# Graph attention and mixture of experts on one core: the adjacency matrix cast in the transfer, with GpSimd issuing both halves ahead of its powers

## Chip, cores and metric

The kernel runs on one core of a Trainium2 chip, which it has to itself. The metric is the device time of one execution in microseconds, as the median of several runs. Engines are named as in the profile: PE (TensorE), DVE (VectorE), ACT (ScalarE), POOL (GpSimd), SP (SyncE, which only issues transfers here).

## What is computed

Two layers over x (2048 tokens, 512 wide), each added to its input. The first is graph attention over an adjacency matrix of 2048 x 2048 zeros and ones, with 16 heads of 32:

```python
x = x + gnn(layernorm(x), adj)
x = x + ffn(layernorm(x))          # router, 8 experts (top 2), shared feed-forward part

def gnn(x, adj, W_seq, a1, a2, W_out, b_out):
    seq = (x @ W_seq).reshape(N, H, DH)
    score1 = einsum('nhd,d->hn', seq, a1)
    score2 = einsum('nhd,d->hn', seq, a2)
    scores = leaky_relu(score1[:, :, None] + score2[:, None, :], 0.2)
    attn = softmax(scores + (1.0 - adj)[None] * -65500.0, axis=-1)
    hidden = einsum('hij,jhd->ihd', attn, seq).reshape(N, D_IN)
    return elu(hidden @ W_out + b_out)
```

A row of the adjacency without any neighbour attends to all tokens evenly.

## The kernel before

leaky_relu has two slopes, so the exponential of a score is a product of a factor of the row token and one of the column token, with one pair of factors on either side of zero. For each head the kernel therefore makes a 0/1 mask "score above zero" and adds up, with PE, the masked values with one pair of factors and the unmasked with the other. The mask (fp8, 2048 x 1024 per unit) is ANDed with the adjacency (fp8, holding -1 and 0, `adj8`, as words `adjw`). A unit is one head and one half (1024) of the rows: 32 units, in 8 pairs of heads, k = 0 to 3 within a pair (head k % 2, half k // 2).

**Setup** (up to about 100 us in the profile). SP loads the constants, W (two pieces), x (four groups of four tiles of 128 tokens) and then the adjacency, 32 pieces of 128 x 1024 floats, through five buffers `adj_in` (lines 192 to 207). ACT and DVE cast them to fp8 in turn (`cast`, lines 223 and 356), 16 pieces each. At the same time DVE centres W, takes the row statistics (`stats`), GpSimd raises the variances to -0.5 in four powers (`root`, line 292), PE transposes W and x and projects x (`project`, line 505, 12 products of 512 columns a tile, with a high and a low part of both operands), ACT splits off high parts (`high_x`) and copies the projected tiles scaled by the power (`copy_v`, line 215, which waits for the power of its group), DVE makes the low parts (`low_x`). PE's `scores` makes both scores of a group, `scores_to_tokens` and `scores_to_rows` turn them; ACT copies the rows (line 265), stores them to memory and loads one row spread over all partitions, `s1b` (lines 267 to 273). DVE ORs the adjacency tiles (`any_neighbour`, lines 424 to 428), PE sums these over the partitions (`degrees`, line 550), and DVE writes flags for rows without neighbours into the adjacency (`apply_empty_rows`, lines 435 and 437). Each engine has its own instruction order, written out by hand; semaphores join them.

**Loop** (to 487.86 us). For each unit DVE compares 6 of the 16 column tiles with the row (line 794) and masks them (`mask_own`, line 802), ACT compares the other 10 (a steep sigmoid, line 730), which DVE masks (`mask_acts`, line 809). PE multiplies (lines 956 and 960) once `m_ready` says that the masks are there. DVE collects the sums from PSUM (`collect`, line 816), GpSimd scales and adds them (`combine`, lines 901 and 906). GpSimd also makes the value products of the next heads (`products`, lines 891 and 893), ACT their high part (`split_high`, line 738), DVE the low (`low_values`, line 823). There are four mask buffers, `MB = 4`. In round k, DVE waits for unit k, collects it, compares and masks its own part of unit k+4, and masks ACT's part of unit k+3.

After the loop come the output projection and the second layer, to the end of the kernel; neither is touched.

## Time and profile before

| | us |
|---|---|
| median of 3 runs | 1058.4 (1056.38 to 1060.91) |
| profiled execution | 1060.79 |
| its span | 1058.9 |
| PE busy | 1006.7 (95%) |
| DVE busy | 803.9 (76%) |
| ACT busy | 666.5 (63%) |
| POOL busy | 251.5 (24%) |
| first attention unit begins | 99.76 |
| output projection begins | 487.86 |

Busy times are of the profiled execution. A busy PE is not a PE at its peak, since matmuls overlap. Where a shape stands beside a row, it is partitions x elements. In a timeline an entry in square brackets gives how long the engine was idle before, and what released it. Lines are those of the kernel before.

### The profile page before, as it was taken

The page shows a single profiled execution, that of the slowest core. Times are in us where ns is not written, and L with a number is a line of the kernel's source. Part 1 is how long each engine was busy: PE and PEld are TensorE (multiplying, and loading weights), DVE is VectorE, ACT ScalarE, POOL GpSimd, SP SyncE. Part 2 cuts the span into 40 slices and gives each one's busy share as a digit, 9 for nine tenths or more (in the row PEclk, how much of TensorE's full clock was granted, in tenths as well). Part 3 has the DMA queues.
Part 4 walks back from the last instruction along what each step waited for, and adds up shares of the span by engine and source line. Part 5 has one row for each costly group of instructions (what it writes and reads, how often), then busy time and mean ns, then how long its engine had stood idle before and what let it go on. Part 6 is the DMA issues. An engine that isn't in the chain of part 4 may idle for free.

```text
span 1058.9 us, 27195 instructions
## 1 busy us (share of the span) xinstructions
PE 1006.7 (95%) x11256; PEld 890.0 (84%) x11256; DVE 803.9 (76%) x1197; ACT 666.5 (63%) x990; POOL 251.5 (24%) x271
## 2 busy tenths in 40 slices
PE   5996889999999999999899999999999999989998
PEld 4875889999999999997677888888888877778887
DVE  6776899999999999993699433448775668975554
ACT  2668999999989889933356333344454546655431
POOL 1103124334333443363331000000065000006500
PEclk9996999999999999999899999999999999999999
DMA  8781111111111111623635000020063124453242
GB/s 301 249 313 40 41 62 43 45 61 42 43 52 52 42 43 52 225 67 132 229 116 208 1 1 1 1 80 1 26 207 117 50 80 131 130 158 112 85 134 99
DMA packets 53778, 102.45 MB, mean 97 GB/s; under 512 B 6161, under 2 KB 26257, under 8 KB 53138
## 3 DMA queue, kind: packets, MB, share of 16 engines
q1 hardware_dynamic: 47666, 82.83, 23.6%
q0 software_dynamic: 3072, 8.39, 2.5%
q10 hardware_dynamic: 2928, 9.57, 2.4%
q8 instruction: 90, 1.47, 0.6%
q14 instruction: 22, 0.18, 0.1%
HBM read 74.69 MB, written 26.08 MB: 95 GB/s over the span
## 4 chain that ended last, share of the span: by engine, by line
PE 47%; issue 2%; DVE 2%; DMA 1%; POOL 1%; ACT 0%; SPq 0%; POOLq 0%; DVEq 0%; ACTq 0%
PE bank L1758 16%; PE bank L1291 16%; PE bank L668 3%; PE bank L1835 2%; PE bank L1786 1%; PE bank L1787 1%; PE bank L1789 1%; DMA xs<-sorted_latent_rows 1%; PE bank L1805 1%; PE bank L1779 1%; PE bank L1743 1%; PE bank L1741 1%; PE bank L665 1%; PE bank L1740 1%; DVE acc_rest L1492 0%
## 5 line engine op out<-in xcount | busy, mean ns | idle before, releaser
L730 ACT ACTIVATE arena<-arena 128x1024 fp8e4<-128x1024 f32 x320 | 336.6, 1136 | 2.5 <-ACT arena L722 1.6
L956 PE MATMUL bank<-arena 128*128 128x132 f16 x4096 | 285.6, 222 | 19.0 <-DVE arena L816 7.6
L956 PEld LDWEIGHTS bank<-arena 128*128 128x128 fp8e4 x4096 | 246.6, 98 | 20.8 <-issue 8.6
L1291 PE MATMUL bank<-xt,up_parts 128*128 128x512 f32 x768 | 186.2, 391 | 0.0
L1758 PE MATMUL bank<-down_parts,h_parts 128*128 128x512 f32 x768 | 184.5, 389 | 0.1
L960 PE MATMUL bank<-arena 128*128 128x66 f16 x4096 | 173.5, 196 | 0.0
L794 DVE TENSOR_SCALAR arena<-arena 128x1024 uint8<-128x1024 f32 x192 | 167.8, 940 | 2.7 <-DMA arena<-s_rows 2.7
L1758 PEld LDWEIGHTS bank<-down_parts,h_parts 128*128 128x128 f32 x768 | 143.9, 188 | 30.5 <-issue 0.5
L1291 PEld LDWEIGHTS bank<-xt,up_parts 128*128 128x128 f32 x768 | 142.3, 188 | 28.6 <-ACT relu_sb L1240 0.2
L960 PEld LDWEIGHTS bank<-arena 128*128 128x128 fp8e4 x4096 | 154.9, 98 | 0.0
L1265 DVE TENSOR_TENSOR relu_sb<-relu_sb 128x512 f32<-128x512 f32 x64 | 44.4, 693 | 118.0 <-ACT relu_sb L1240 110.9
L1240 ACT ACTIVATE relu_sb<-bank 128x512 f32<-128x512 f32 x64 | 38.3, 598 | 148.6 <-PE bank L1291 143.8
L901 POOL TENSOR_TENSOR arena<-arena 128x264 f32<-128x264 f32 x64 | 43.1, 694 | 214.3 <-DVE arena L809 195.5
L809 DVE TENSOR_TENSOR arena<-arena 128x2560 uint32<-128x2560 uint32 x32 | 90.2, 2819 | 2.6 <-ACT arena L730 2.5
L1259 ACT CAST down_parts<-down_sb 128x512 fp32r<-128x512 f32 x64 | 39.9, 623 | 72.4 <-PE bank L1758 66.7
L1712 POOL DMA_INDIRECT sorted_latent_rows<-latent,slot_idx x32 | 35.0, 1094 | 208.7 <-DVE slot_idx L1578 190.9
L1280 DVE TENSOR_TENSOR down_parts<-down_sb,down_parts 128x512 fp32r<-128x512 f32 x64 | 44.2, 691 | 50.1 <-ACT down_parts L1259 46.8
L1724 POOL DMA_INDIRECT y_gathered<-sorted_expert_rows,slot_idx x32 | 32.6, 1020 | 156.3 <-DMA sorted_expert_rows<-expert_y 135.4
L891 POOL TENSOR_TENSOR arena<-arena 128x512 f32 (+1 forms) x32 | 50.2, 1569 | 59.3 <-ACT arena L220 31.4
L802 DVE TENSOR_TENSOR arena<-arena 128x1536 uint32<-128x1536 uint32 x32 | 56.3, 1758 | 1.1
L816 DVE TENSOR_REDUCE arena<-bank 128x198 f32<-128x396 f32 (+1 forms) x96 | 44.2, 516 | 9.8 <-PE bank L956 9.8
L668 PE MATMUL bank<-wo_parts,hT 128*128 128x512 f32 x192 | 50.2, 412 | 0.0
(231 smaller groups left out, 1403.9 us busy)
## 6 DMA issues: line engine op xcount, KB each, us to landing
hid<-in_adjT SPq DMA_DIRECT2D x32, 512.0 KB, 5.8
arena<-s_rows SPq DMA_DIRECT2D x30, 512.0 KB, 3.7
sorted_latent_rows<-zeros SPq DMA_DIRECT2D x1, 4992.0 KB, 18.5
xs<-sorted_latent_rows SPq DMA_DIRECT2D x39, 128.0 KB, 2.1
sorted_expert_rows<-expert_y SPq DMA_DIRECT2D x39, 128.0 KB, 1.7
arena<-in_x SPq DMA_DIRECT2D x4, 1024.0 KB, 10.8
xr<-in_x SPq DMA_DIRECT2D x16, 256.0 KB, 2.8
up_sb<-in_upT ACTq DMA_DIRECT2D x1, 4096.0 KB, 14.0
```

The lines of the kernel that those rows point to most:

```text
L668: last = nc.tensor.matmul(bank[2 + t % 2][:, :], hT[:, t % 2, a, k, :], wo_parts[:, b, k, :], start=False, stop=(n == len(terms) - 1))
L730: last = nc.scalar.activation(m8[:, k, j, :], s1b[:, k % 2, :], ACT.Sigmoid, bias=bias_now[:, k % 2, j:j + 1], scale=STEEP, saturate=False)
L794: last = nc.vector.tensor_scalar(mu8[:, k, j, :], s1b[:, k % 2, :], neg_s2[:, 2 * p + k % 2, j:j + 1], float(ONE8), ALU.is_gt, ALU.mult)
L802: nc.vector.tensor_tensor(mw[:, k, 0:DVE_J, :], mw[:, k, 0:DVE_J, :], adjw[:, 0:DVE_J, cols], ALU.bitwise_and).then_inc(own_masked, 1)
L809: nc.vector.tensor_tensor(mw[:, k, DVE_J:, :], mw[:, k, DVE_J:, :], adjw[:, DVE_J:, cols], ALU.bitwise_and).then_inc(m_ready, 1)
L816: last = nc.vector.reduce_sum(sums[:, k % 2, t0:t0 + n, :], bank[3 * (k % 2) + g][:, 0:n * WV].rearrange("p (t s c) -> p t c s", t=n, s=2) ...
L891: nc.gpsimd.tensor_tensor(vtmp[:, :, c * W1:c * W1 + DH], vh, val[:, :, bass.ds(h, 1)].to_broadcast([P, T, DH]), ALU.mult)
L956: last = nc.tensor.matmul(o, m8[:, k, j, i * P:(i + 1) * P], vs[:, b, j, :], start=(j == 0), stop=(j == T - 1))
L960: nc.tensor.matmul(od, adj8[:, ja, (k // 2) * IC + i * P:(k // 2) * IC + (i + 1) * P], vs[:, b, ja, :].rearrange("p (s c) -> p s c", s=2)[ ...
L1265: nc.vector.tensor_tensor(r, r, r, ALU.mult).then_inc(sq_ready, 1)
L1291: last = nc.tensor.matmul(bank[6 + s % 2][:, :], sa[:, s % 2, a, k, :], xt[c][:, b, k, :], start=(i == 0), stop=(i == len(mm) - 1))
L1758: last = nc.tensor.matmul(ob[t][:, :], hhl[:, s % 2, a, t * P:(t + 1) * P], sb_[:, s % 2, b, :], start=(n == 0 and (a, b) == TERMS[0]), st ...
```

## The change

The setup is rewritten around a transfer that casts, and the loop's order shifts by one unit.

- The adjacency is no longer loaded as floats and cast. GpSimd, after its constants and a wait for the second group of x (`x_loaded[1]`), issues eight transfers that read floats and write fp8 straight into `adj8`: 512 rows by 1024 columns each, first the four of the first half of the columns, then the four of the second, and only then its four powers. `cast`, `adj_in` and all semaphores of the casts are gone. The adjacency now holds +1 and 0; the flags set the sign bit everywhere and -1 in rows without neighbours.
- SP loads W in four pieces and x in groups of 2, 2, 4, 4 and 4 tiles; the small constants are issued by ACT. W is centred by ACT, piece by piece, and transposed piece by piece.
- The rows of scores go to memory in three stores issued by SP. The first holds only what the first two heads need of the first half; the two spread rows are loaded right behind it.
- PE's order: `scores_to_rows` ahead of `project(7)`, `degrees(1)` ahead of `project(13, 14, 15)`. Unit 0 begins with the first 12 token tiles (`T_A = 12`) of three of its row tiles, the last 4 follow; the values of the first head are made in two parts, 12 tiles by GpSimd and 4 by DVE.
- DVE applies the empty rows of the first half before the first compare, and in the loop compares three units ahead (not four) and masks ACT's part two ahead (not three). ACT's compares shift likewise. In the first pair the mask buffers are used in the order 0, 2, 1, 3.

The core of the diff:

```diff
-            for q in range(HALVES):
-                if q >= AB:
-                    sp.wait_ge(cast_by_act if (q - AB) % 2 else cast_by_dve, (q - AB) // 2 + 1)
-                sp.dma_start(adj_in[:, q % AB, :], adjT[(q % T) * P:(q % T + 1) * P, (q // T) * IC:(q // T + 1) * IC]
-                             ).then_inc(adj_loaded[q % AB], 16)
+            sp.wait_ge(st_copied, 6)
+            sp.dma_start(s1_dram[0:2, 0:IC], s1_rows[0:2, 0:IC]).then_inc(s1_stored, 16)
+            sp.wait_ge(s1_stored, 16)
+            for k in range(2):
+                sp.dma_start(s1b[:, k, :], s1_dram[k:k + 1, 0:IC].to_broadcast([P, IC])).then_inc(s1_staged[k], 16)
...
+            def load_adjacency(half):
+                cols = slice(half * IC, (half + 1) * IC)
+                for g in range(AG):
+                    pool.dma_start(adj8[:, 4 * g:4 * g + 4, cols],
+                                   adjT[512 * g:512 * g + 512, cols].rearrange("(j p) i -> p j i", p=P)
+                                   ).then_inc(adj_loaded[half], 16)
+
+            pool.wait_ge(x_loaded[1], 16)
+            load_adjacency(0)
+            load_adjacency(1)
             for g in range(4):
                 root(g)
...
-                cast_up_to(8)
+                dve.wait_ge(adj_loaded[half], 16 * AG)
                 step(nc.vector.tensor_tensor(anyw, adjw[:, 0:4, words], adjw[:, 4:8, words], ALU.bitwise_or))
...
+            high_x(0, 1, 2, 3)
             copy_v(0)
-            high_x(2, 3)
             act.wait_ge(wa_in_psum, 1)
             nc.scalar.copy(wa[:, :, 0:2 * H], WA_BANK[:, 0:KD * 2 * H].rearrange("p (k s) -> p k s", k=KD)).then_inc(wa_high, 1)
...
-            project(8, 9, 10, 11, 12, 13, 14, 15)
+            project(8, 9, 10, 11, 12)
             degrees(1)
+            project(13, 14, 15)
...
-                        if k or not first:
-                            dve.wait_ge(unit_in_psum, 4 * p + k + 1)
-                            collect(p, k)
-                        if not last:
-                            if k >= 2:
-                                low_values(p + 1, k % 2)
-                            compare(p + 1, k)
-                            mask_own(p + 1, k)
-
-                        if k == 0:
-                            mask_acts(p, 3)
-                        elif not last:
-                            mask_acts(p + 1, k - 1)
+                        dve.wait_ge(unit_in_psum, 4 * p + k + 1)
+                        collect(p, k)
+                        if not last and k >= 2:
+                            low_values(p + 1, k % 2)
+                        if not last or k == 0:
+                            compare(p + (k + 3) // 4, (k + 3) % 4)
+                            mask_own(p + (k + 3) // 4, (k + 3) % 4)
+                        if not last or k < 2:
+                            mask_acts(p + (k + 2) // 4, (k + 2) % 4)
...
                 dve.wait_ge(seq_in_psum, 8)
                 compare(0, 0)
-                cast(26)
                 mask_own(0, 0)
-                cast(28, 30)
                 any_neighbour(1)
-                low_values(0, 0)
-                mask_acts(0, 0)
-                dve.wait_ge(seq_in_psum, T)
                 compare(0, 1)
                 mask_own(0, 1)
+                mask_acts(0, 0)
+                low_first(0, slice(0, T_A))
+                apply_empty_rows((2,))
+                products_first(slice(T_A, T))
+                low_first(1, slice(T_A, T))
+                apply_empty_rows((3,))
+                compare(0, 2)
+                mask_own(0, 2)
                 low_values(0, 1)
                 mask_acts(0, 1)
```

## Rows read from the trace of the kernel before

**Rows 1.** windows of setup and loop: busy us by engine, clock, DMA share, GB/s
```profile
0.00:99.70 99.70, 76.20 (x384) 62.13 (x384) 67.82 (x122) 59.74 (x83) 11.65 (x19) 0.94 0.70 239
...
150.00:430.00 280.00, 276.68 (x6132) 275.80 (x6130) 279.18 (x275) 267.24 (x268) 108.63 (x120) 1.00 0.14 48
```

**Rows 2.** PE's timeline: start us, us, line, operation, count
```profile
17.82 0.47 PE L511 MATMUL bank<-w_high,x_high 128*128 128x512 f32 x1 [1.08 <-DVE x_low L353]
...
31.02 0.40 PE L511 MATMUL bank<-w_high,x_high 128*128 128x512 f32 x1
...
33.75 1.47 PE L502 MATMUL bank<-arena 128*128 128x128 f32 x12
...
99.76 0.27 PE L956 MATMUL bank<-arena 128*128 128x132 f16 x1 [7.23 <-DVE arena L809]
...
106.63 0.67 PE L960 MATMUL bank<-arena 128*128 128x66 f16 x16
...
108.07 0.67 PE L960 MATMUL bank<-arena 128*128 128x66 f16 x16
...
487.86 0.73 PE L665 MATMUL bank<-bout_parts,ones_r 1*128 1x512 f32 x2
```

**Rows 3.** waits, 60 to 100 us: waiter, awaited, us, times, longest
```profile
POOL arena L891 <- ACT arena L220: 31.4, 1, 31.4
```

**Rows 4.** groups up to 99 us: line, operation, count, busy, mean ns
```profile
L227 ACT ACTIVATE arena<-hid 128x1024 fp8e4<-128x1024 f32 x16 | 16.7, 1056 | 3.5 <-DMA hid<-in_adjT 3.1 <-ACT arena L265 0.5
...
L361 DVE TENSOR_SCALAR arena<-hid 128x1024 fp8e4<-128x1024 f32 x16 | 10.8, 687 | 0.8 <-DMA hid<-in_adjT 0.8
...
L437 DVE TENSOR_TENSOR arena<-arena 128x2048 uint32<-128x2048 uint32 x2 | 4.6, 2293 | 0.1
...
L424 DVE TENSOR_TENSOR hid<-arena 128x1024 uint32<-128x1024 uint32 x2 | 2.4, 1219 | 0.0
...
L435 DVE TENSOR_SCALAR arena<-bank 128x512 uint8<-128x512 f32 x2 | 1.4, 683 | 0.0
```

**Rows 5.** DVE's timeline: the first compare, and four rounds of the loop
```profile
74.38 4.07 DVE L794 TENSOR_SCALAR arena<-arena 128x1024 uint8<-128x1024 f32 x6 [2.69 <-DMA arena<-s_rows]
...
201.65 1.38 DVE L816 TENSOR_REDUCE arena<-bank 128x198 f32<-128x396 f32 x3
202.95 1.34 DVE L823 TENSOR_TENSOR arena<-arena 128x1056 f16<-128x1056 f32 x1
204.21 6.08 DVE L794 TENSOR_SCALAR arena<-arena 128x1024 uint8<-128x1024 f32 x6
210.33 1.76 DVE L802 TENSOR_TENSOR arena<-arena 128x1536 uint32<-128x1536 uint32 x1
212.00 2.82 DVE L809 TENSOR_TENSOR arena<-arena 128x2560 uint32<-128x2560 uint32 x1
214.74 1.38 DVE L816 TENSOR_REDUCE arena<-bank 128x198 f32<-128x396 f32 x3
...
226.17 1.38 DVE L816 TENSOR_REDUCE arena<-bank 128x198 f32<-128x396 f32 x3
...
238.24 1.38 DVE L816 TENSOR_REDUCE arena<-bank 128x198 f32<-128x396 f32 x3
...
248.62 1.38 DVE L816 TENSOR_REDUCE arena<-bank 128x198 f32<-128x396 f32 x3
```

**Rows 6.** windows of the transfers, columns as in rows 1
```profile
5.00:25.00 20.00, 12.41 (x76) 11.65 (x77) 15.69 (x40) 5.17 (x9) 2.07 (x2) 1.00 1.00 382
...
25.00:62.00 37.00, 37.00 (x208) 30.36 (x208) 28.07 (x57) 24.18 (x38) 3.75 (x5) 1.00 0.75 236
```

**Rows 7.** GpSimd's first power, and its nearest transfer (ns min/median/max)
```profile
14.84 1.05 POOL L294 TENSOR_TENSOR arena<-arena 128x4 f32<-128x4 f32 x1 [13.63 <-DVE arena L346]
...
L1712 POOL DMA_INDIRECT sorted_latent_rows<-latent,slot_idx x32: 959/970/1502, 764.9 to 816.4; - x32
```

**Rows 8.** ACT's timeline: the issue of the store of the rows
```profile
61.06 0.40 ACTq L267 DMA_DIRECT2D s_rows<-arena  x1
```

More of the change, by code:

```diff
@@ L256, in setup_act @@
-            cast(11)
+            copy_scores(3)
             copy_v(5)
-            copy_scores(3)
-            cast(13, 15)
+            copy_rows(0, 1)
             copy_v(6)
-            cast(17)
-            copy_v(7)
-            for c in range(4):
-                act.wait_ge(st_in_psum, 5 + c)
-                nc.scalar.copy(s1_rows[:, c * 512:(c + 1) * 512], ROW_BANK[c][0:H, :]).then_inc(st_copied, 1)
-            act.wait_ge(st_copied, 8)
-            act.dma_start(s1_dram[:, :], s1_rows).then_inc(s1_stored, 16)
@@ L268, in setup_act @@
-            cast(19)
-            copy_v(8)
-            cast(21)
-            act.wait_ge(s1_stored, 16)
-            for k in range(2):
-                act.dma_start(s1b[:, k, :], s1_dram[k:k + 1, 0:IC].to_broadcast([P, IC])).then_inc(s1_staged[k], 16)
-            copy_v(9)
+            copy_rows(2, 3)
             act.wait_ge(expin_ready, 1)
@@ L347, in stats @@
                                         ALU.add).then_inc(var_ready, 1)
+            def stats(g):
+                row_stats(*range(4 * g, 4 * g + 4))
+                variances(g)
             def low_x(*tiles):
@@ L354, in low_x @@
                                             xhi[:, t, :, :].bitcast(f32), ALU.subtract).then_inc(xl_ready, 1)
-            def cast(*even):
-                for q in even:
-                    dve.wait_ge(adj_loaded[q % AB], 16 * (q // AB + 1))
-                    src, dst = cast_source(q)
-                    nc.vector.tensor_scalar(dst, src, -1.0, None, ALU.mult, saturate=False).then_inc(cast_by_dve, 1)
             def diagonal_a():
@@ L554, in setup_pe @@
             pe.wait_ge(consts_loaded, 48)
-            pe.wait_ge(w_centred, 1)
-            transpose_w()
+            for c in range(KD):
+                transpose_w(c)
             transpose(0, 1)
-            pe.wait_ge(w_ready, 1)
+            pe.wait_ge(w_ready, KD)
             project(0)
@@ L735, in split_high, with split_first @@
                 def split_high(p, b):
-                    act.wait_ge(prod_ready, 2 * p + b + 1)
+                    act.wait_ge(prod_ready, 2 * p + b + 2)
                     nc.scalar.copy(vs[:, b, :, 0:WD], vtmp).then_inc(hi_copied, 1)
+                def split_first(part, tiles):
+                    act.wait_ge(prod_ready, part + 1)
+                    nc.scalar.copy(vs[:, 0, tiles, 0:WD], vtmp[:, tiles, :]).then_inc(hi_copied, 1)
                 def body(p, last):
                     for k in range(4):
-                        act.wait_ge(unit_in_psum, 4 * p + k + 1)
-                        if not last:
-                            if k >= 2:
-                                split_high(p + 1, k % 2)
-                            compare(p + 1, k)
+                        if not (last and k):
+                            act.wait_ge(unit_in_psum, 4 * p + k + 1)
+                        if not last and k >= 2:
+                            split_high(p + 1, k % 2)
+                        if not last or k == 0:
+                            compare(p + (k + 3) // 4, (k + 3) % 4)
@@ L831, in split_low, with body @@
                     nc.vector.tensor_scalar(ones_r[0:1, :], ident2[0:1, :], 0.0, 1.0, ALU.mult, ALU.add).then_inc(wo_low, 1)
-                def body(p, last=False, first=False):
+                def body(p, last=False):
                     for k in range(4):
@@ L950, in _, with products @@
                         pe.wait_ge(m_ready, 4 * p + k + 1)
-                        for i in range(IT):
+                        def products(i, tokens):
                             g, slot = GROUP_OF[i]
@@ L963, in _ @@
                                         start=False, stop=False, skip_group_check=True)
+                            return last
+                        ahead = [t0 for t0, n in GROUPS] if p == 0 and k == 0 else []
+                        for i in ahead:
+                            if i == ahead[-1]:
+                                pe.wait_ge(v_copied, T - 1)
+                            products(i, range(T_A))
+                        if ahead:
+                            pe.wait_ge(lo_ready, 2)
+                        for i in ahead:
+                            products(i, range(T_A, T))
+                        for i in range(IT):
+                            if i not in ahead:
+                                last = products(i, range(T))
                         last.then_inc(unit_in_psum, 1)
```

326 lines of the change are left out of this document (165 added, 161 removed).

## Prediction, before the changed kernel was run

> **What bounds the kernel now.** I read the stages first, then the chain inside each. The windows by stage show two regimes [rows 1]: up to 99.70 us no engine is full (PE 76.20, DVE 67.82, ACT 59.74 us of it), from 150 to 430 us PE and DVE are both full (276.68 and 279.18 of 280). In the setup the end is set by a chain: 99.76 us is where the first attention unit begins, after 7.23 us of idle PE [rows 2]. Behind it stands GpSimd, which could not multiply the values of the first head before the last tile was copied by ACT: 31.4 us of waiting for line 220 [rows 3]. ACT is late with those copies because PE is late with its 16 projections, and both ACT and DVE also cast the adjacency, 16 halves each [rows 4].
>
> In the loop one unit costs PE eight tiles of 1.44 us (106.63 to 108.07), 11.52 us [rows 2]. DVE's round of collect, compare, mask has four lengths, read from collect to collect [rows 5]: 13.09 (k=2, with low values and with GpSimd's products beside it: its six compares take 6.08), 11.43 (k=3), 12.07 (k=0, products again), 10.38 (k=1). The sum is 46.97 for four units, 0.9 more than PE's 46.1. DVE is the bound on average, and the masks of a unit are finished three units ahead, so a long round is evened out by a short one. The loop ends at 487.86, where the output projection begins [rows 2]. From there both kernels are the same.
>
> **The change part by part.** The times below are on the clock of the profiled run (1060.8 us, span 1058.9). It stands 2.4 over the median of 1058.4, and I take the difference of the sum over to the median.
>
> *Casts.* 16 on ACT at 1.056 and 16 on DVE at 0.687 go: 16.7 and 10.8 us of work [rows 4], none of it on the path by itself while PE is full, but it held up the copies and the order of DVE.
>
> *Start.* W comes in four quarters and first in the queue, its centring goes to ACT, tile by tile. In the new order, with 128x512 on DVE at 0.68 [rows 4]: first quarter of W landed at 4.6, four quarters of statistics of 1.1 to 9.1, the small diagonal and two x statistics to 10.8, four low parts of W to 13.2 at 0.62 apart (ACT's high parts are ready by 11.8), the first low part of x to 14.0. So the first projection is at 14.0, an estimate, instead of 17.82 [rows 2]: -3.8.
>
> *The eight transfers.* GpSimd waits for the second group of x, estimated at 9.4 us: 2 MB behind the first byte at the 382 GB/s of 5 to 25 us [rows 6], begun 1.4 us earlier. Then it issues eight transfers of 512 rows, and only then the first power (1.05) [rows 7]. ACT stands at the copy of tile 0 until that power is there; behind it are the score columns, x tiles 4 and on, so all of PE. PE would want those columns at 25.5: 14.0, two projections of 2.73, the products for the columns (3.6), five tiles of x at 0.4 (twelve transposes in 1.47 [rows 2]) and their waits, 0.4. ACT and DVE take 1.5 from the power to the columns, so the power is wanted at 24.0. So there is cover for 24.0 - 9.4 - 1.05 = 13.5 us of issuing, 1.7 us each. No row shows a direct transfer from GpSimd. The nearest is an indirect one of 128 rows, 0.97 [rows 7]. Bounds: 0.97 (rows cost nothing) and 3.9 (four times as many rows, all in proportion). I take 1.94, double, as part of the 0.97 must be fixed and indices fall away: 15.5 us, 2.0 us over the cover. Below nothing isn't possible: the powers cannot come before their variances at 20.
>
> The row only shows 0.97 for 128 rows. The Trainium skill (DMA: Bandwidth & Descriptors, Anatomy of one DMA) calls descriptor generation small and variable, with many descriptors to be had before the cost shows. By that the 2.0 us would be nothing and the result 1049.0; no run here shows it.
>
> *To the first compare.* From the first projection to the issue of the rows' store it was 61.06 - 17.82 = 43.2 [rows 2, 8], with PE full (37.00 of 37 us [rows 6]). One projection (2.73, 31.02 to 33.75 [rows 2]) now comes later, and two of four row copies, estimated at 0.5 each: 39.5. So the store is issued at 14.0 + 39.5 + 2.0 = 55.5. In the kernel before, it was 13.3 from that issue to the compare at 74.38 [rows 5, 8], beside a busy queue; the store is now a sixteenth of the size and I take 10: 65.5. On DVE the empty rows come before: with a projection and the degrees to go for PE these end near 60.2, two flags of 0.68 + 2.29 [rows 4] behind 59.3, then the scaling, 66.1. So the first compare starts at 66 instead of 74.38.
>
> *From there to round 0 of the loop* DVE has in its order: compare 4.07 and own mask 1.67, three ORs of 1.22, compare and own mask again, mask of ACT's part 2.73, low values of 12 tiles 0.95, an empty-row flag 3.0, products and low values of 4 tiles 1.0, a flag 3.0, third compare beside products 5.7 and own mask 1.67, low values 1.25, ACT's mask 2.73 [rows 4, 5]. That is 37.2. For the handing of the 4 tiles over ACT, and for GpSimd's products beside the second compare, I add 2.2. Round 0 begins at 105.4. PE: projections end near 87, degrees of the second half wait some 2 us for the ORs; unit 0 needs PE from about 89 to 102 and is covered.
>
> *The loop itself changes.* Compares are made three units ahead instead of four, and ACT's part is masked two ahead instead of three. The masks of unit k+2 are finished by round k's last instruction, and round k+1 starts only when unit k+1 is done, a unit that could start only with round k. Rounds and units go in step: each step costs the longer of the two. With 0.14 (estimated) for handing over in the rounds where DVE would be the shorter: 13.09 + 11.66 + 12.07 + 11.66 = 48.5 a pair instead of 46.97. For seven pairs 339.5. From the last pair's start three units (34.6) and 0.9 for eight transposes ahead of the last (twelve take 1.47 [rows 2]): 35.5. End: 105.4 + 339.5 + 35.5 = 480.4, against 487.86: -7.4. **Predicted: 1058.4 - 7.4 = 1051.0.** Gross, the setup gives some 18 us and the loop takes 11 back.
>
> *The data.* 16.8 MB and 3 MB of x from 9.4 us at 382 GB/s: second half landed at 61.5, wanted by DVE at 66 + 5.7 = 71.7; first half near 39, wanted at 43. Covered, while the stream holds 320 GB/s. Bounds: 382, and the 236 of 25 to 62 us [rows 6], where the casts held the transfers back. I take 382, since reading is what fills the engines in those rows (share 1.00).
>
> **The rivals.**
> *B, the powers come late (0.16).* At 3.9 us each, 31.2 us of issuing is 17.7 over the cover, 15.7 more than forecast: 1066.7. It decides from 1.7 us each; the gain is gone at 2.9. For it: 512 rows against 128, ACT in order. Against: the fixed part. The Trainium skill (SBUF — State Buffer, Who interferes with whom) adds that GpSimd can't write descriptors while DVE runs a two-port operation. Here DVE's compares are longer beside GpSimd's products (6.08 against 4.07 [rows 5]), so the two do hinder each other; in the window of issuing DVE mostly reads PSUM or makes statistics.
>
> *C, the casting stream is slower than the plain one (0.20).* At 236 GB/s the second half lands at 93.7, 22 us behind its want: 1058.4 - 7.4 + 22 = 1073. It decides under 320 GB/s and the gain is gone at 290. For it: no row shows a casting transfer. Against: the rows written are a quarter of those read. This is the slower side in its clearest form.
>
> *D, no stepping (0.13).* If DVE's rounds even out after all (less contention, since PE idles and ACT has less to do), the loop keeps 46.97 a pair: 1040.
>
> *E, the clock falls in the loop (0.07).* In step, PE idles 1.6 us in each pair. After the stall before 99.76 three tiles took 6.87 (99.76 to 106.63) instead of 4.32 [rows 2], and the granted clock was 0.94 over that stage, 1.00 in the loop [rows 1]. If each such gap does the same: 7 x 2.55 = 17.9, 1068.9. Against: PE's gaps of 0.9 in a pair today leave the clock at 1.00.
>
> **How the numbers follow.** The forecast has 0.44, with 1046 to 1057 as its own range (issuing 1 to 2.4 us, first compare give or take 4). 0.5% is 5.3 us and about what a measurement of this kernel can tell from no change. Faster by more (under 1053.1): two thirds of the forecast, all of D: 0.45. Within (to 1063.7): the rest of the forecast, mild forms of B, C and E: 0.27. Slower: 0.28, strong forms of B, C and E. The range that leaves out 2 in 10 goes from D to just under C: 1040 to 1072.
>
> **What would show it.** In the profile after: the first power of GpSimd near 26 and ACT's copy of tile 0 right behind it (B: near 40); DVE not waiting for the adjacency at the first OR (C: a wait on the transfer of in_adjT, of some 20 us at the second half); first compare near 66, unit 0 near 89; collects of DVE in the loop 13.1, 11.7, 12.1, 11.7 apart with short waits for PE (D: 47.0 in four); granted clock 1.00 from 150 to 430 (E: lower); output projection at 480. A new wait that none of these has, say DVE for the copied tiles in the second half of the setup, would make the sum wrong.

## Result

| | before | after |
|---|---|---|
| median | 1058.72 us (1056.38 to 1062.01, 9 runs) | 1064.05 us (1062.19 to 1065.14, 9 runs) |
| profiled execution | 1060.79 | 1063.28 |
| its span | 1058.9 | 1061.5 |
| first projection | 17.82 | 13.38 |
| first compare on DVE | 74.38 | 69.19 |
| first attention unit begins | 99.76 | 90.00 |
| output projection begins | 487.86 | 491.83 |

The ratio is 1.0041, with an interval of 1.0027 to 1.0056. 1051.0 was predicted, so the sign was wrong. The attention begins 9.8 us earlier and ends 4.0 us later. Behind the output projection the two profiled executions differ by 1.5 us (572.9 and 571.5), with nothing changed there; the medians are 5.3 us apart.

Two stages of the changed kernel, the start of the loop and the steady loop, in the columns of [rows 1]:

```profile
88.00:150.00 62.00, 52.50 (x1058) 51.49 (x1057) 54.61 (x58) 58.33 (x60) 18.55 (x21) 0.92 0.13 43
150.00:430.00 280.00, 267.51 (x5865) 265.86 (x5864) 264.59 (x261) 251.50 (x250) 99.91 (x111) 0.99 0.13 44
```

In the loop neither PE (267.51) nor DVE (264.59) is full any more, where both had all but filled the 280 us before [rows 1]. The waits from 150 to 430 us say why (waiter, awaited, us in all, times, longest):

```profile
DVE arena L816 <- PE bank L965: 13.3, 11, 3.1
ACT arena L722 <- PE bank L965: 13.3, 6, 3.9
PE bank L965 <- DVE arena L809: 12.5, 11, 1.8
```

DVE waits for PE at its collect (line 816), and PE waits for DVE's last mask (line 809), eleven times each: they take turns. DVE's own timeline shows the rounds, from collect to collect (line 816). The first five collects here are the first pair with a wait for ACT in it (line 823), the last is one steady pair later:

```profile
107.80 1.38 DVE L816 TENSOR_REDUCE arena<-bank 128x198 f32<-128x396 f32 x3
122.02 1.39 DVE L816 TENSOR_REDUCE arena<-bank 128x198 f32<-128x396 f32 x3 [3.52 <-PE bank L965]
133.54 1.39 DVE L816 TENSOR_REDUCE arena<-bank 128x198 f32<-128x396 f32 x3 [1.24 <-PE bank L965]
136.81 1.26 DVE L823 TENSOR_TENSOR arena<-arena 128x1056 f16<-128x1056 f32 x1 [1.88 <-ACT arena L730]
...
148.13 1.38 DVE L816 TENSOR_REDUCE arena<-bank 128x198 f32<-128x396 f32 x3
162.65 1.39 DVE L816 TENSOR_REDUCE arena<-bank 128x198 f32<-128x396 f32 x3 [3.07 <-PE bank L965]
...
211.45 1.39 DVE L816 TENSOR_REDUCE arena<-bank 128x198 f32<-128x396 f32 x3 [0.43 <-PE bank L965]
```

From 162.65 to 211.45 a pair takes 48.80 us, against 46.97 before [rows 5], and its four rounds 11.87, 11.95, 13.03 and 11.95. The first pair, 107.80 to 162.65, takes 54.85, and its rounds 14.22, 11.52, 14.59 and 14.52. PE beside it:

```profile
108.03 0.27 PE L965 MATMUL bank<-arena 128*128 128x132 f16 x1 [5.67 <-DVE arena L809]
109.01 1.95 PE L965 MATMUL bank<-arena 128*128 128x132 f16 x16
113.75 1.10 PE L965 MATMUL bank<-arena 128*128 128x132 f16 x16
...
148.36 0.27 PE L965 MATMUL bank<-arena 128*128 128x132 f16 x1 [3.33 <-DVE arena L809]
149.34 1.95 PE L965 MATMUL bank<-arena 128*128 128x132 f16 x16
```

Behind both idle stretches (5.67 and 3.33 us) the same sixteen products take 1.95 instead of 1.10 us: TensorE is at 1.2 GHz there (granted clock 0.50 from 108 to 113) and back at 2.4 from 113 to 115 (0.99). And GpSimd, which was the question of the change:

```profile
10.53 6.22 POOL L304 DMA_DIRECT2D arena<-in_adjT  x8 [9.32 <-DMA arena<-in_x]
21.29 1.04 POOL L293 TENSOR_TENSOR arena<-arena 128x4 f32<-128x4 f32 x1 [4.54 <-DVE arena L349]
...
45.20 0.38 POOL L299 PARTITION_ALL_REDUCE arena<-arena  x1 [5.93 <-issue]
53.70 0.59 POOL L315 TENSOR_TENSOR arena<-arena 128x1 f32<-128x1 f32 x1 [8.12 <-issue]
60.55 0.39 POOL L299 PARTITION_ALL_REDUCE arena<-arena  x1 [6.26 <-issue]
```

Eight issues take 6.22 us together, 0.78 each, and the first power waits 4.54 us for its variances (line 349), not for them. Behind the powers stands what the prediction didn't price: a power, an all-reduce, a power, an all-reduce, with 5.93, 8.12 and 6.26 us between them in which GpSimd waits for nothing that the profile shows. DVE stands behind the last of them:

```profile
60.98 0.43 DVE L403 TENSOR_TENSOR arena<-arena 128x256 f32<-128x256 f32 x1 [7.43 <-POOL arena L299]
...
62.44 0.68 DVE L429 TENSOR_SCALAR arena<-bank 128x512 uint8<-128x512 f32 x1
...
69.19 4.06 DVE L794 TENSOR_SCALAR arena<-arena 128x1024 uint8<-128x1024 f32 x6
```

### The profile page after: what moved, and what is told of

It is laid out like the page before. It is cut to its first block, busy times and chain, and to the rows that moved or that the text cites. A ratio compares the mean times of both kernels' runs of the same rounds, so it can differ in the third digit from the quotient of the medians.

```text
span 1061.5 us, 27178 instructions
## 1 busy us (share of the span) xinstructions
PE 1009.1 (95%) x11256; PEld 889.8 (84%) x11256; DVE 795.0 (75%) x1186; ACT 654.2 (62%) x979; POOL 257.6 (24%) x279
## 4 chain that ended last, share of the span: by engine, by line
PE 46%; issue 2%; DVE 2%; DMA 2%; POOL 1%; ACT 0%; SPq 0%; POOLq 0%; DVEq 0%; ACTq 0%
PE bank L1781 16%; PE bank L1314 16%; PE bank L656 3%; PE bank L1858 2%; DMA xs<-sorted_latent_rows 1%; PE bank L1809 1%; PE bank L1810 1%; PE bank L1812 1%; PE bank L1766 1%; PE bank L1764 1%; PE bank L653 1%; PE bank L1802 1%; PE bank L1828 1%; DMA sorted_expert_rows<-expert_y 1%; PE bank L1763 1%
## 5 line engine op out<-in xcount | busy, mean ns | idle before, releaser
L897 POOL TENSOR_TENSOR arena<-arena 128x512 f32 (+2 forms) x32 | 46.8, 1462 | 40.6 <-ACT arena L221 15.0
```

The source lines that it names most:

```text
L897: nc.gpsimd.tensor_tensor(vtmp[:, tiles, c * W1:c * W1 + DH], vh[:, tiles, :], val[:, tiles, bass.ds(h, 1)].to_broadcast([P, n, DH]), ALU. ...
```

## Experiments

The theory after the result: the setup's gain is real, and the loop's shorter look-ahead takes more than all of it (S). Rivals: the transfers or their order cost it; GpSimd's chain costs it (G); PE's clock costs it (K). All ratios are against the kernel before, measured beside each run on the same chip.

| run | us | ratio (interval) | output projection at |
|---|---|---|---|
| e1 four ahead | 1051.06 | 0.9905 (0.9880 to 0.9929) | 479.90 |
| e2 before, in step | 1076.0 | 1.0142 (1.0115 to 1.0169) | 505.91 |
| e3 reduces together | 1059.7 | 0.9986 (0.9966 to 1.0007) | 486.42 |
| e4 second half behind the powers | 1074.24 | 1.0128 (1.0103 to 1.0152) | |
| e5 four ahead, reduces together | 1046.37 | 0.9852 (0.9821 to 0.9884) | 476.32 |
| e6 fillers | 1063.99 | 1.0029 (1.0015 to 1.0042) | 492.38 |
| e7 before, cast in the transfer | 1053.51 | 0.9926 (0.9901 to 0.9951) | 480.28 |
| e8 second half last | 1074.52, one run | | |
| e9 sixteen transfers | 1065.56, one run | | |
| e10 both halves behind the powers | 1081.51, one run | | |
| e11 layout only | 1064.22 | 1.0035 (1.0009 to 1.0061) | 491.41 |
| e12 e5 with fillers | 1049.12 | 0.9879 (0.9836 to 0.9922) | 477.10 |
| e13 ACT relieved | 1059.23 | 0.9993 (0.9982 to 1.0005) | 486.80 |
| e14 ACT relieved, fillers | 1059.63 | 0.9988 (0.9975 to 1.0002) | 487.98 |

### The look-ahead: e1, e2, e11

e1 is the changed kernel with the loop of the kernel before (its diff in DVE's order; ACT and GpSimd likewise). So that the mask buffers can be used in plain order, x and its parts lie in two halves of eight tiles.

```diff
-BUF = (0, 2, 1, 3)
+BUF = (0, 1, 2, 3)
...
-                            compare(p + (k + 3) // 4, (k + 3) % 4)
-                            mask_own(p + (k + 3) // 4, (k + 3) % 4)
-                        if not last or k < 2:
-                            mask_acts(p + (k + 2) // 4, (k + 2) % 4)
+                            compare(p + 1, k)
+                            mask_own(p + 1, k)
+                        if k == 0:
+                            mask_acts(p, 3)
+                        elif not last:
+                            mask_acts(p + 1, k - 1)
```

> The changed kernel with the loop's look-ahead of before: DVE compares four units ahead and masks ACT's part three ahead, ACT and GpSimd likewise, mask buffers in plain order, for which the x tiles lie in another order in the same memory. The setup is left as changed. Theory S (the shorter look-ahead makes PE and DVE go in step and that takes the setup's gain back): four units take 47.0 us again instead of 48.8, seven pairs give back 12.7 us, the output projection begins near 479 and the time is about 1052, under the kernel before. Rival T (the loss is in the first units and in slower clocks, not in the look-ahead): pairs stay near 48.8 and the time within 2 us of 1064.

Measured 1051.06 us (1048.70 to 1051.49). From 183.20 to 230.16 a pair takes 46.96 us, as before. In the waits of the loop DVE's for PE is gone, and PE waits about as rarely as before (e1, 150 to 430 us):

```profile
PE bank L972 <- DVE arena L821: 4.5, 6, 0.9
```

e2 is the opposite edit, the changed kernel's loop in the kernel before.

> The kernel before with the loop of the changed kernel alone: compares three units ahead, ACT's part masked two ahead; setup untouched. Theory S: four units take 48.8 us instead of 47.0, the first unit stays near 99.8, and the time is 1058.7 + 7 x 1.8 = about 1071 (less, down to 1068, if less DVE work stands ahead of the first units). Rival T: about 1059, no change beyond noise.

Measured 1076.0: 15 us slower by the ratio, 5 over the expected 1071. In the profile 2.4 us of it lie ahead of the loop (the first unit begins at 102.15 instead of 99.76), where nothing was edited; the rest was not followed up. Its loop waits like the changed one's:

```profile
DVE arena L817 <- PE bank L948: 13.7, 12, 3.0
PE bank L948 <- DVE arena L810: 13.7, 11, 1.8
```

e11 has e1's layout of x and the loop of the changed kernel.

> Control for the run with four ahead: the changed kernel with that run's layout of x (two halves of eight tiles, mask buffers in plain order) and its own look-ahead of three. If the gain of 13 us came from the look-ahead, this one stays at 1064, ratio 1.002 to 1.006. If the layout gave it, 1051.

Measured 1064.22 us: the layout does nothing. So one unit of look-ahead is worth 13.0 us in one kernel and about 15 in the other (1.42% of 1060), more than the 11 that the prediction charged, and it alone turns a gain of 1% into a loss. Four ahead doesn't free the start of the loop from ACT, though: in e1 DVE waits 6.76 us for ACT's compares (line 722) ahead of its first collect and 2.22 for its copy (line 730) behind it, against 2.51 us for ACT at this place in the kernel before. What it would give to take that away as well, no run shows.

### The cast by itself: e7

The kernel before with `adj_in` and all casts taken out, and the eight transfers of the change in front of the powers. The flags for empty rows are those of the change; order and loop are those of before.

```diff
-            for q in range(HALVES):
-                if q >= AB:
-                    sp.wait_ge(cast_by_act if (q - AB) % 2 else cast_by_dve, (q - AB) // 2 + 1)
-                sp.dma_start(adj_in[:, q % AB, :], adjT[(q % T) * P:(q % T + 1) * P, (q // T) * IC:(q // T + 1) * IC]
-                             ).then_inc(adj_loaded[q % AB], 16)
...
+            pool.wait_ge(x_loaded[1], 16)
+            load_adjacency(0)
+            load_adjacency(1)
             for g in range(4):
                 root(g)
```

> The kernel before with only the transfer changed: the adjacency read as floats and written as fp8 by eight transfers that GpSimd issues in front of its powers, no casts on ACT and DVE, the flags for empty rows as in the changed kernel. Order of everything else and the loop are those of the kernel before. Theory: the issue of the eight (6.2 us in the changed kernel) ends at 17.7 and the first power comes 2.9 us later than the 14.84 of the kernel before, which PE feels little; without the casts ACT's copies and DVE's order run earlier, so that the first attention unit begins near 93 to 95 instead of 99.76, and as the loop keeps its four units of look-ahead, the whole gain is seen at the end: 1052 to 1054, ratio 0.994 to 0.996. Rival: the setup is bound by the chain of scores, store, broadcast and all-reduces alone, in which no cast lies: first unit near 99, ratio 0.998 to 1.000.

Measured 1053.51 us; the theory holds (the first unit was expected at 93 to 95 and begins at 92.21). The output projection begins at 480.28, e1's at 479.90: all the rest of the rewritten setup, which brings the first projection forward by 4.0 us (17.34 in e7, 13.31 in e1) and takes the store of the rows apart, is worth 0.4 us in these two profiles. The medians lie 2.5 us apart, with intervals of the ratios that overlap. Both stand behind the same link, GpSimd's second all-reduce. Here it is in e7:

```profile
60.35 0.39 POOL L289 PARTITION_ALL_REDUCE arena<-arena  x1 [8.01 <-issue]
```

It begins at 61.41 in e1 and at 60.35 here, and the first compare at 70.06 and 70.17. How much the rest of the setup gives once this link is out of the way was not measured on its own.

### GpSimd's chain: e3, e5

e3 is the changed kernel with both all-reduces next to each other:

```diff
             largest(0, slice(H, H + 1))
+            largest(1, slice(0, H))
             pool.wait_ge(var_ready, 5)
             nc.gpsimd.tensor_tensor(gfac[:, 1:2], gfac[:, 0:1], inv_root, ALU.pow).then_inc(std_ready, 1)
-            largest(1, slice(0, H))
```

> The changed kernel with GpSimd's two all-reduces behind one another and the fifth power (of the scale factor) behind both, instead of between them. Theory G (each change between powers and all-reduces costs GpSimd 6 to 8 us without an instruction, and this chain, not PE, the transfers or the row store, sets DVE's first compare): exponents of DVE begin near 54 instead of 61, the fifth power comes near 61, the first compare starts at 66 to 67 instead of 69.2, the time falls by 2 to 3 us to about 1061.5. Rival: the gaps are the reduce's own latency, whatever stands before it; then the second all-reduce still ends near 61 and the time stays at 1064.

Measured 1059.7 us, 4.3 under the changed kernel, where 2 to 3 were expected. GpSimd in e3:

```profile
52.99 0.55 POOL L299 PARTITION_ALL_REDUCE arena<-arena  x1 [7.07 <-DVE arena L396]
60.95 1.07 POOL L316 TENSOR_TENSOR arena<-arena 128x1 f32<-128x1 f32 x1 [7.41 <-issue]
```

The second all-reduce now waits for its data (line 396) and nothing else, and begins at 52.99, where the rival had it end near 61; the change back to a power, 7.41 us, happens beside DVE's work. The first compare begins at 65.31 instead of 69.19, behind PE's degrees (DVE waits 3.43 us for line 535 ahead of the flags), which is the next link. Whether an all-reduce behind another has a gap of its own is not shown: the wait of 7.07 us is long enough to hide one. e5 puts this edit and the look-ahead of e1 together.

> The changed kernel with both of the earlier edits: the loop's look-ahead of the kernel before (compares four units ahead, own layout of x so that the mask buffers are in plain order) and the two all-reduces back to back with the fifth power behind them. Theory: the two losses lie one behind the other, so the gains add. The look-ahead alone gave 1064.05 - 1051.06 = 13.0, the reduces alone 1064.05 - 1059.7 = 4.3: 1046.8 or a ratio of about 0.987 to 0.988. Rival: the loop of four ahead can absorb a late first round, so that what the first round gains is not seen at the end: 1051, ratio 0.990 to 0.993, as with the look-ahead alone.

Measured 1046.37 us (1044.24 to 1047.16): the gains add, and this beats both kernels, by 1.5% and 1.7%.

### What lengthens the gaps: e4, e8, e10

e4 puts `load_adjacency(1)` behind the four powers, e10 both halves, e8 the second half behind the last all-reduce.

> The changed kernel with the four transfers of the second half issued behind the four powers. Theory: the eight issues took 6.2 us in all and ended 4.5 us before the first power could start, so nothing waits for them; the power stays at 21.3, the second half lands near 60 instead of 57.3, wanted at 75, and the time stays within 1.5 us of 1064. Rival (transfers issued ahead of the powers hold up the x tiles or the powers): faster than the changed kernel by 2 us or more, x groups land earlier.

e4 took 1074.24 us, 10 more than the changed kernel, a miss. Its transfers of the second half are issued from 40.67 to 43.73, and its gaps are longer:

```profile
52.98 0.38 POOL L299 PARTITION_ALL_REDUCE arena<-arena  x1 [9.24 <-issue]
64.88 0.59 POOL L315 TENSOR_TENSOR arena<-arena 128x1 f32<-128x1 f32 x1 [11.53 <-issue]
72.36 0.39 POOL L299 PARTITION_ALL_REDUCE arena<-arena  x1 [6.89 <-issue]
```

The last all-reduce begins 11.8 us later than in the changed kernel, and so does DVE's first compare (81.00): that is where the 10 us are.

> The changed kernel with the four transfers of the second half issued behind the last all-reduce, so that the queue is empty from about 38 us on while GpSimd goes from powers to all-reduce, back, and to all-reduce again. Theory Q: what GpSimd waits for at these changes of kind is hindered by the transfers that run beside it: with an empty queue the gaps fall from 5.9, 8.1 and 6.3 us to under 5 each, and the exponents come 5 us earlier or more. Rival R: the gaps have a length of their own and do not feel the queue: 6 to 8 us each as before, and the longer ones of the run with the second half behind the powers (9.2, 11.5, 6.9) belong to the change from a transfer's issue to an all-reduce, not to the queue. Under either the second half lands some 19 us after its issue, near 76 to 82, by up to 7 us later than it is wanted: 1064 to 1071.

In e8 the transfers' share is 0.11 from 40 to 60 us, where it is 1.10 from 38 to 57 in the changed kernel, and the gaps are these:

```profile
45.74 0.38 POOL L299 PARTITION_ALL_REDUCE arena<-arena  x1 [5.73 <-issue]
53.27 0.76 POOL L314 TENSOR_TENSOR arena<-arena 128x1 f32<-128x1 f32 x1 [7.16 <-issue]
60.32 0.39 POOL L299 PARTITION_ALL_REDUCE arena<-arena  x1 [6.29 <-issue]
```

Rival R holds for the empty queue, and theory Q falls in its size: an empty queue takes away 0.2, 1.0 and 0 us (most of the third gap lay beside an empty queue in the changed kernel already, from some 57 us on). A change of kind has a price of its own here, 5.7 to 7.2 us. The 10 us of e8's 1074.5 are another thing: the second half lands too late, and DVE waits 9.82 us for it at the first OR of that half.

> The changed kernel with all eight transfers issued behind the fourth power instead of in front of the first. The powers wait for their variances only (the last begins at 38.3), so the issue begins at 39.3 and ends at 45.5; the first half lands near 66, the second near 86, against 37.5 and 57. The first OR, wanted by DVE at about 45, waits some 20 us, and the second, wanted at 75, some 11 more. Expected: first compare near 88 to 90, time 1085 to 1090. This is the price of the other order, with no rival about its sign; what it tells is whether putting the transfers first costs the powers anything: if the powers begin at 21.3, 24.3, 31.9, 38.3 here too, give or take 1, the issue of the eight was free; if they begin 4 us earlier or more, it was not.

Measured 1081.51 us, below what was expected, with the first compare at 87.44. The powers begin at 19.39, 22.29, 31.48 and 37.86, against 21.29, 24.28, 31.88 and 38.27 in the changed kernel. The 2 us at the first two are not the price of the issue in front of them: e13 (below) has the same eight issues there, and its powers begin at 19.49, 22.49, 30.09 and 36.48. What differs is PE's first projection. Its products are 0.43 us apart up to 17.4 in the changed kernel and 0.23 apart in e13; PE, changed kernel and then e13:

```profile
13.95 0.63 PE L496 MATMUL bank<-w_low,x_high 128*128 128x512 f32 x1
14.37 0.63 PE L496 MATMUL bank<-w_high,x_low 128*128 128x512 f32 x1
...
13.75 0.40 PE L497 MATMUL bank<-w_low,x_high 128*128 128x512 f32 x1
13.99 0.40 PE L497 MATMUL bank<-w_high,x_low 128*128 128x512 f32 x1
```

The setup is the same in both, and the granted clock reads 1.00 in both; why one execution begins at half the pace is open. The first compare doesn't feel it (69.19 and 69.11). So the eight issues in front were free. But the gaps of e10, all three now beside a full queue (share 1.12):

```profile
55.72 0.38 POOL L299 PARTITION_ALL_REDUCE arena<-arena  x1 [10.64 <-issue]
67.19 0.59 POOL L315 TENSOR_TENSOR arena<-arena 128x1 f32<-128x1 f32 x1 [11.09 <-issue]
78.81 0.39 POOL L299 PARTITION_ALL_REDUCE arena<-arena  x1 [11.03 <-issue]
```

Beside a full queue of casting transfers the gaps lie between 5.9 (changed kernel) and 11.5 us (e4), beside an empty one between 5.7 and 7.2. Rival R explains the first gap of e4 and e10, which stands behind an issue, but not the others, which don't. Against e8 those are longer by 3.9 and 4.7 us in e10 and by 4.4 in e4's second. These are single executions, and they show the longer gaps beside the stream of casting transfers; why it left the first gap of the changed kernel at 5.93 is open. Plain transfers go with longer gaps too: 8.05, 7.37 and 7.28 in the kernel before (share 0.81 from 40 to 60 us).

### The price of an issue: e9

Sixteen transfers of 256 rows for eight of 512 (`AG = 8`).

> The changed kernel with sixteen transfers of 256 rows in place of eight of 512; the data are the same. The disputed cost by itself: what GpSimd pays for one issue. Eight took 6.22 us, 0.78 each. Theory P (the price goes with the rows or with the bytes): 0.39 each, 6.2 us in all. Theory F (a fixed price per transfer): 0.78 each, 12.4 us in all, ending near 23; the first power then waits 2 us longer, which is inside the cover of 13.5 us. Either way the first compare stays within 1 us of 69.2 and the time within 3 us of 1064.

Sixteen issues take 11.73 us, 0.73 each:

```profile
10.95 11.73 POOL L304 DMA_DIRECT2D arena<-in_adjT  x16 [9.73 <-DMA arena<-in_x]
```

Theory F: half the rows cost nearly the same, 0.73 for 0.78. The first power begins at 22.71, right behind, 1.4 us later than in the changed kernel, the first compare at 70.21.

### The first pair: e6, e12, e13, e14

Three causes were possible for the 54.85 us of the first pair: PE's clock, ACT, DVE's own order. e6 keeps PE at work with products that nobody reads:

```diff
+                def filler(n):
+                    for _ in range(n):
+                        nc.tensor.matmul(bank[6][:, 0:WV], adj8[:, 0, 0:P], vs[:, 0, 0, :], start=True, stop=True)
...
+                        if p == 0 and k == 1:
+                            filler(90)
...
+                        if p == 1 and k == 0:
+                            filler(50)
```

> The changed kernel with matmuls that write to a bank nobody reads: 90 before unit 1 and 50 before unit 4, on a PE that waits for masks there. Theory K (clock): the slow tiles behind these two waits (1.95 us instead of 1.09 in unit 1, and again in the unit behind 148.36) come from PE's clock falling in the idle stretch; with PE kept at work the tiles behind take 1.1 to 1.5 and the kernel gains 3 to 6 us: 1058 to 1061, granted clock from 88 to 150 us near 1.00 instead of 0.92. Rival: the slow tiles are the price of the data being handed over (weights of masks that arrive one by one), and the granted clock has nothing to do with it: no gain, 1064, or a loss of 1 to 3 us where a filler is still running when the masks are there.

Measured 1063.99 us, no gain, although the clock did what theory K asked. From 100 to 125 us it was granted in full (0.86 in the changed kernel), and the tiles of unit 1 took 1.10. DVE's round 0 is 11.94 long (108.55 to 120.49) instead of 14.22. Two rounds later the 2.3 us are gone (e6):

```profile
100.00:125.00 25.00, 25.00 (x531) 24.86 (x529) 23.69 (x27) 25.00 (x25) 5.81 (x7) 1.00 0.14 45
...
137.56 1.26 DVE L823 TENSOR_TENSOR arena<-arena 128x1056 f16<-128x1056 f32 x1 [4.16 <-ACT arena L730]
...
148.88 1.38 DVE L816 TENSOR_REDUCE arena<-bank 128x198 f32<-128x396 f32 x3
```

DVE waits 4.16 us for ACT's copy of the next values (line 730), where it waited 1.88. So ACT was a second bound right behind the clock, and theory K, which held for the clock, fails in the time. In the changed kernel ACT compares without a pause from 99.96 to 158.90 (no idle over 0.3 us):

```profile
99.96 25.05 ACT L722 ACTIVATE arena<-arena 128x1024 fp8e4<-128x1024 f32 x24
125.31 10.51 ACT L722 ACTIVATE arena<-arena 128x1024 fp8e4<-128x1024 f32 x10 [0.20 <-ACT arena L714]
135.72 1.06 ACT L730 CAST arena<-arena 128x1056 f16<-128x1056 f32 x1
```

e13 takes six compares from ACT ahead of the loop (three rows of unit 1, three of unit 2; one copy of zeros writes the three, so that this part of the masks is left out). e14 does that and has e6's fillers.

```diff
-                compare_rows(1, DVE_J + 6, T, BUF[1])
-                compare(0, 2)
+                skip_rows(DVE_J + 6, T - 1, BUF[1])
+                compare_rows(1, T - 1, T, BUF[1])
...
+                skip_rows(DVE_J, DVE_J + 3, buf(0, 2))
+                compare_rows(2, DVE_J + 3, T, buf(0, 2))
```

> The changed kernel, in which ACT leaves out six of its compares ahead of the loop (three of unit 1, three of unit 2; one copy of zeros writes the three rows instead, so that these masks are zero, which the text says once: this part of the computation is left out). ACT has some 5 us less to do before 115 us. Theory A (ACT's backlog is what the fillers ran into): DVE's wait of 1.88 us for ACT's split in the round behind 133.5 goes, and the round ends 2 us earlier; the wait for PE behind unit 1's slow tiles stays. 1061 to 1063, ratio 1.000 to 1.003. Rival: the later waits for PE take it all: 1064, ratio 1.004.

> The same relief of ACT (six compares left out) together with the matmuls that keep PE at work before units 1 and 4. Theory A: now the 1.5 us that the fillers won in unit 1 and the 4.2 us of waiting for ACT that took them both go: 4 to 6 us under the changed kernel, 1058 to 1060, ratio 0.998 to 1.000. Theory Z: something else than ACT and the clock stretches the first two pairs (DVE's own order): 1062 to 1064, ratio 1.002 to 1.004.

e13 measured 1059.23 us, 4.8 under the changed kernel and better than expected. e13's DVE:

```profile
107.62 1.38 DVE L824 TENSOR_REDUCE arena<-bank 128x198 f32<-128x396 f32 x3
...
145.57 1.38 DVE L824 TENSOR_REDUCE arena<-bank 128x198 f32<-128x396 f32 x3
157.51 1.39 DVE L824 TENSOR_REDUCE arena<-bank 128x198 f32<-128x396 f32 x3 [0.50 <-PE bank L973]
```

The first pair takes 49.89 us instead of 54.85. The wait for ACT is gone, and with it PE's stall before unit 4 shrinks from 3.33 to 1.76 us and its clock stays up (granted in full from 125 to 150 us, 0.94 in the changed kernel), so the round behind 145.57 takes 11.94 instead of 14.52. That is the mechanism: a copy on ACT that came 1.9 us late lengthened PE's stall from 1.8 to 3.3 us, and behind the longer stall the slow tiles cost 2.6 more. Round 0 stays long (13.42 us), behind the same stall of 5.67 ahead of unit 1; that part is the clock alone, and e6 took it away (11.94). e14 measured 1059.63 us, in line with its expectation. Its first pair is 49.37; the fillers' gain of 1.5 us up to its fourth collect is given back mostly before unit 4, where the filler makes DVE wait 1.44 us for PE instead of 0.50.

> Four ahead, both all-reduces together, and the fillers on PE ahead of unit 1 and unit 4. With four ahead DVE is the bound of the loop and PE has time to spare, so a lower clock for two tiles is hidden: expected the same as without fillers, 1046.4 give or take 1.5, ratio 0.984 to 0.988. Rival: in the stage from 88 to 150 us the granted clock was still 0.94 without fillers; if the slow tiles there lie on the chain, the fillers gain 1 to 4 us: 1042 to 1045.

1049.12 us against e5's 1046.37, on another chip; the ratios are 0.9879 and 0.9852, and their intervals overlap. The fillers bring nothing there either, and the rival's 1042 to 1045 is out.

## Why the prediction was wrong, point by point

Two steps of the sum failed, and they lie in different stages. The loop was charged 48.5 us for each of its seven pairs, so that ACT's backlog and the clock in the first of them stood at nothing; that pair took 54.85, 6.35 us more. And the path to the first compare went over the degrees and left GpSimd's second all-reduce out, which had ended near 60 us in the kernel before and still did; the compare began at 69.19 instead of 66, and round 0 2.4 us late. The remaining 2.7 us are pairs and an end that were each a little too cheap.

*The start* (14.0) was right: 13.38. That the first projection itself then ran at half the pace in this execution cost the powers 2 us and the first compare nothing (e10 and e13 above).

*The eight transfers* were priced at 1.94 us each, 15.5 in all, 2.0 over the cover. They took 0.78 each, 6.22 in all, under even the lower bound of 0.97 that the indirect transfer gave [rows 7]; the term of 2.0 is 0. The slip here, on the cautious side, was to take an indirect transfer of 128 rows as a floor and let rows count: e9 shows that 256 rows more cost 0.05 us. The Trainium skill (DMA: Bandwidth & Descriptors, Anatomy of one DMA) was the better guide; by its rule the 2.0 us would be nothing, and the trace agrees. Rival B is out.

*The store* was expected at 55.5 and issued at 54.73. *The data*: from 25 to 55 us the queue wrote 107 GB/s of fp8, which is four times as much read, 428 GB/s, more than the 382 of plain transfers [rows 6]. There is no wait for the adjacency in the changed kernel. Rival C is out.

*To the first compare* the sum said 66, and it was 69.19. The step put the flags behind the degrees, at 59.3. In DVE's order the exponents stand before them, and these waited 7.43 us for GpSimd's second all-reduce; the flags began at 62.44. The three gaps on GpSimd were in the trace of before too, hidden there by a later store of the rows. GpSimd's timeline, kernel before:

```profile
44.30 0.38 POOL L300 PARTITION_ALL_REDUCE arena<-arena  x1 [8.05 <-issue]
52.05 0.59 POOL L306 TENSOR_TENSOR arena<-arena 128x1 f32<-128x1 f32 x1 [7.37 <-issue]
59.92 0.39 POOL L300 PARTITION_ALL_REDUCE arena<-arena  x1 [7.28 <-issue]
```

The last one ends at 60.3 before and at 60.9 after: this chain didn't move. (It began 3 us later, with a fourth power that ended at 39.3 instead of 36.2, and its three gaps were together 2.4 us shorter.) The sum moved every other chain ahead and didn't ask what else had ended at 60. e3 shows the price. The Trainium skill (GPSIMD Engine Reference, Instruction dispatch) has a wait of this kind: the first call to freshly loaded code on GpSimd pays about 6 us with no instruction visible. The trace's 5.73 to 7.16 us beside an empty queue agree roughly, the 11 us of e10 do not. Whether loading code is what happens in the gaps, no run here shows: in e8's second gap (46.2 to 53.2 us) the trace has no transfer of any kind.

*To round 0*: 39.4 us were charged and 38.6 taken. Round 0 began at 107.80, 2.4 after the forecast, all from the step above.

*The loop itself.* The stepping was seen and its size in the steady state was right: 48.5 forecast, 48.80 measured, waits in the rounds that were named. Rival D is out. What failed is that all seven pairs were charged alike. The first took 54.85, 6.35 more. Against the steady rounds its first is 2.35 us longer, behind PE's stall of 5.67 ahead of unit 1 and the half clock after it; that is the clock alone. Its third and fourth are 1.6 and 2.6 longer: ACT comes to the loop with a backlog and, with one unit of slack less, passes it on, so that DVE waits, PE stalls for longer, and the clock falls again. With ACT relieved (e13) the pair took 49.89, 4.96 less. The prediction had the last link as rival E, but as something that each steady gap would do; the steady gaps of up to 1.8 us leave the clock at 1.00 (160 to 430 us). (By its own rounds PE idles 2.4 us in each pair and not 1.6; the longest gap is the 1.6.) ACT's compares in the prelude weren't in the sum at all.

*The end*: 162.65 + 6 x 48.5 + 35.5 = 489.2 by the forecast's terms, measured 491.83, so 2.7 more, of which the six pairs are 2.3 (five of 48.8 and a last one of 49.4) and the end 0.4.

Together 2.4 + 6.35 + 2.7 = 11.4, the distance from 480.4 to 491.83. Of the 13.05 us between 1051.0 and 1064.05 that leaves 1.6: the part behind the projection took 1.5 less, and the profiled execution stands 0.8 under its median where that of before stood 2.4 over, which makes 3.2.

*Gross figures.* "The setup gives some 18 us and the loop takes 11 back" was wrong in both halves. The setup gives 8.0 (e1: 479.90 against 487.86) and the loop takes 12 (491.83 against 479.90). The 18 counted as gain that one unit's masks move out of the setup; this work does not vanish, the loop does it. That last reading is an argument from the order of the instructions; no run takes the two apart.

## What to carry to other kernels

Slack between engines that take turns was worth more here than the start it was sold for: with one unit of look-ahead less, every round costs the longer of the two engines (48.8 us a pair for 47.0), and a late copy of one engine becomes a stall and a lower clock of another. When a change pulls several chains forward, list every chain that ended near the old time, GpSimd's gaps between kinds of instruction among them, since the one left standing sets the gain. And price a backlog: an engine below 100% over the loop (ACT 251.5 of 280 us) can still be the bound of its first rounds.

## What the hardware showed

- A casting transfer from GpSimd costs it 0.73 us of issuing with 256 rows (e9) and 0.78 with 512, and the stream of them ran at 107 GB/s written, 428 read.
- GpSimd's change between a power and an all-reduce costs 5.7 to 7.2 us beside an empty queue (e8), and up to 11.5 beside a full one (e4, e10). Between two powers behind one another there is none (e7: 2.12 us for both, 1.0 to 1.1 each). With the same eight transfers behind the powers the gaps were 10.6 to 11.1, with them in front 5.9 to 8.1.
- Behind a stall of 5.67 or 3.33 us PE ran the next tiles at half speed (1.95 for 1.10 us, granted clock 0.50); behind stalls of up to 1.8 us it did not (1.76 in e13, and the loop from 160 us on, granted clock 1.00).
- The granted clock in the rows doesn't tell everything: from 13.4 to 17.4 us it reads 1.00 in the changed kernel and in e13, and the same products stand 0.43 us apart in one and 0.23 in the other.
